# A transformer layer with routed experts on one core: gate and up in three passes of split numbers, small VectorE work moved to ScalarE and GpSimd

## The chip, the cores and the metric

One NeuronCore of a Trainium2 chip runs the whole layer as one program. Its engines run side by side and meet at semaphores: TensorE (PE) multiplies, VectorE (DVE) and ScalarE (ACT) work on SBUF and PSUM, GpSimd (POOL) on SBUF, SyncE (SP) issues most DMAs. The metric is device time in microseconds, lower is better. Three runs of the kernel before took 2507.96, 2511.35 and 2512.93 us, median 2511.35.

## The reference

The input x has shape 8 x 1024 x 256, float32. The layer is attention with a residual and a layer norm, then a routed feed-forward with a residual and a layer norm.

```python
q = einsum('bld,dhk->blhk', x, Wq)            # 16 heads of 64
latent = einsum('bld,dc->blc', x, Wkv_down)   # 64 wide
k, v = latent @ Wk_up, latent @ Wv_up         # per head
attn = softmax(where(causal, q @ k.T / 8, min))
x = layernorm(x + (attn @ v) @ Wout)
# routed feed-forward: T = 8192 tokens, E = 32 experts, C = 320 slots each
probs = softmax(xt @ w_router); top1 = argmax(probs); gate = probs[top1]
pos = cumsum(onehot(top1))[top1] - 1          # rank among the expert's tokens
buf[top1 * C + pos] = xt                      # dropped where pos >= C
g, u = buf @ w_gate, buf @ w_up               # 256 x 256 per expert
y = (silu(g) * u) @ w_down
x = layernorm(xt + where(pos < C, y[slot] * gate, 0))
```

## The kernel before

**Attention.** The loop runs over 64 pairs of heads (gp, eight per batch b, p = gp % 8) and in each over 12 slots t, a slot being 128 keys against a block of 512 queries. In a slot TensorE makes scores by keys (`turned_scores`, L699 and L702), scores by rows for the row maxima of the next pair (`row_scores`, L674), and every second slot probabilities times values (`values`, L722). VectorE takes the row maxima (`row_max`, L1117 and L1121), ScalarE the exponentials (L964), GpSimd masks the diagonal (L479) and adds up the probabilities (L494 to L504). Every engine's program is written out in one order by hand. What belongs to the batch before is put between the slots of the next batch's first pairs: output projection in p = 0 and 1, layer norm in p = 1 and 2, transposed rows and router logits in p = 2, ranks in p = 3, sending rows to the experts' slots in DRAM in p = 4 and 5. The layer norm's steps are `variance` (VectorE, L1191 and L1194), `roots` (GpSimd, L517 to L529) and `normalise` (VectorE, L1199: x1 minus mean, times rstd, four tiles of 128 x 256 at slots (1, 10) and (2, 4)). `count_tiles` (L1240 to L1244) and `destinations` (L1249 to L1257) are VectorE's work in p = 3, slots 9 and 11; `send` (L536) is GpSimd's indirect DMA.

TensorE's float32 products come as two instructions in the trace. Products in F32R come as one; where float32 accuracy is wanted with them, an operand is split into a high part (a cast to F32R) and a low part (the rest), and three passes are added: high by high, low by high, high by low. Queries and latents are made in that way (L621).

**Experts.** When all rows are in DRAM, the loop runs over 32 experts, two to a pair g. TensorE transposes an expert's 320 rows (`transpose_rows`, L879), VectorE copies them to SBUF (`copy_rows`, L1332 and L1333), TensorE makes gate and up in float32 (`gate_and_up`, L891), ScalarE applies silu (`activate`, L1038), VectorE multiplies (`hidden`, L1338), TensorE projects down in five blocks of 128 rows per pair (`down`, L910 and L915), VectorE adds them to the rows and takes their statistics (`add_to_rows`, L1350 to L1364), GpSimd takes the root (`root`, L572 and L575), ScalarE scales (`normalise_out`, L1044), and GpSimd sends the rows to the output (`send_back`, L581). TensorE's order is gate and up of e, transposes of e+2, and after the second expert of a pair the down projection. ScalarE's is the activations of e and, after those of a pair's first expert, `normalise_out` of the pair before.

Weights have eight buffers (`ex_w`, AHEAD = 8), `ex_y` two. SP loads the weights of five experts during the last pair of heads, the other three between the first rows, and then for e = 8 and on:

```python
for e in range(AHEAD, E):
    g = (e - AHEAD) // 2
    sp.wait_ge(ex_sent[g % 2], 16 * NY * (g // 2 + 1))   # output of pair g has landed
    load_rows(e)
    load_weights(e)                                      # gate, up, down: three DMAs
```

Of the kernel before, what the change touches and what calls it, by code (L numbers as in the profile page):

```python
# [16 lines left out]
P = 128  # L17
# [6 lines left out]
def build_layer(nc, x, Wq, Wkv, Wk_up, Wv_up, Wout, w_router, w_gate, w_up, w_down, out):  # L24
# [48 lines left out]

    NADD = 11
# [7 lines left out]
    with ExitStack() as ctx:  # L82
# [23 lines left out]
        fold_lo = sb("fold_lo", [P, KD, NPAIR * P], F32R, attn)  # L106
        future = sb("future", [P, BANK], F32, attn)
# [6 lines left out]
        lat_hi = [sb(f"lat_hi{i}", [P, L], F32R, attn) for i in range(2)]  # L114
        lat_lo = [sb(f"lat_lo{i}", [LD + 1, L], F32R, attn) for i in range(2)]
        lat_keys = [sb(f"lat_keys{i}", [P, NT, LD], F32, attn) for i in range(2)]
        fold_v = sb("fold_v", [P, NPAIR, D], F32, attn)
        q_hl = [sb(f"q_hl{i}", [P, 2, L], F32R, attn) for i in range(2)]
# [52 lines left out]
        EARLY_W = 5  # L171
# [6 lines left out]
        ex_xT = sb("ex_xT", [P, 2, KD, 2 * C], F32, tail)  # L178
# [40 lines left out]
        rstd_ready = sem("rstd_ready")  # L219
        x1_ready = sem("x1_ready")  # L220
# [10 lines left out]
        ex_loaded = [sem(f"ex_loaded{i}") for i in range(AHEAD)]  # L231
        ex_t_full = sem("ex_t_full")
# [34 lines left out]
        for gp in range(PAIRS):  # L267
# [16 lines left out]
            if b and p == 2:  # L284
                for use, t in zip([(hf, kd) for hf in range(2) for kd in range(KD)], (3, 5, 7, 10)):
                    late[t].append(("x1T", b - 1, *use))
                late[11].append(("logits", b - 1))
# [71 lines left out]
        def _(sp):  # L359
# [42 lines left out]
            def load_weights(e):  # L402
                k = e % AHEAD
                for m, w in enumerate((w_gate, w_up, w_down)):
                    sp.dma_start(ex_w[k][:, m], w[e].rearrange("(k p) f -> p k f", p=P)).then_inc(ex_loaded[k], 16)
# [37 lines left out]
        def _(pool):  # L443
# [69 lines left out]
            def roots(b, hf):  # L513

                tiles = slice(hf * HPB, (hf + 1) * HPB)
                pool.wait_ge(var_ready, b * 2 + hf + 1)
                nc.gpsimd.tensor_tensor(rstd[:, tiles], var_eps[:, tiles], minus_half[:, tiles], ALU.pow  # L517
                                        ).then_inc(rstd_ready, 1)
                pool.wait_ge(rstd_ready, b * 2 + hf + 1)
                nc.gpsimd.tensor_tensor(alone[:, 0, tiles], rstd[:, tiles], rstd[:, tiles], ALU.mult  # L520
# [9 lines left out]
                                        ).then_inc(alone_scale, 1)  # L530

# [8 lines left out]
            for gp in range(PAIRS):  # L540
                b, p = divmod(gp, NPAIR)
                for t in range(NSLOT):
# [10 lines left out]
                    if b and (p, t) in ((1, 8), (2, 2)):  # L553
# [6 lines left out]
            for hf in range(2):  # L560
                roots(LAST, hf)
            for i in range(NT):
                send(LAST, i)
# [4 lines left out]
            def root(g):  # L568

                part = slice(g % 2 * NY, (g % 2 + 1) * NY)  # L570
                pool.wait_ge(var_ready, 2 * B + g + 1)
                nc.gpsimd.tensor_tensor(rstd[:, part], var_eps[:, part], minus_half[:, part], ALU.pow  # L572
# [13 lines left out]

            for g in range(E // 2):
                root(g)
                send_back(g)

        @block.tensor
        def _(pe):
# [181 lines left out]
            def count(b):  # L774
                use = ("pos", b)
                bank = take(use)
                pe.wait_ge(onehot_ready, b + 1)
                nc.tensor.matmul(bank[:, 0:NT * E], before_bf[:, :], onehot[:, :, :].rearrange("p t e -> p (t e)"),
# [89 lines left out]
            def transpose_rows(e):  # L868
# [3 lines left out]
                if u == 0:  # L872
                    for k in (e % AHEAD, e % AHEAD + 1):
                        pe.wait_ge(ex_loaded[k], (e // AHEAD + 1) * (16 * (3 + NB)))
# [8 lines left out]
            def gate_and_up(e):  # L883
                g, u = divmod(e, 2)
                pe.wait_ge(ex_t_ready, e + 1)
                for f in range(KF):
                    if e:
                        pe.wait_ge(ex_h_ready[f], e)
                    for m in range(2):
                        for kd in range(KD):  # L890
                            mm = nc.tensor.matmul(turned_ps[f][:, m, 0:C], ex_w[e % AHEAD][:, m, kd, f * P:(f + 1) * P],  # L891
                                                  ex_xT[:, g % 2, kd, u * C:(u + 1) * C],
                                                  start=(kd == 0), stop=(kd == KD - 1))
# [36 lines left out]
        def _(act):  # L930
# [42 lines left out]

            def pass_alone(b, i):
# [36 lines left out]

            for gp in range(PAIRS):
                b, p = divmod(gp, NPAIR)
                for t in range(NSLOT):
# [5 lines left out]
                    for use in EARLY.get((gp, t), []) + LATE[gp, t]:  # L1020
                        if use[0] in STAGES:
                            STAGES[use[0]](*use[1:])
                    if b and p == 3 and t < NT:
                        pass_alone(b - 1, t)
                    if b and (p, t) == (3, 4):
                        gate_exponentials(b - 1)
            copy_heads(PAIRS - 1, 1)
# [11 lines left out]

            def normalise_out(g):  # L1040
# [6 lines left out]

            for e in range(0, E, 2):
                for u in range(2):
                    activate(e + u)  # L1050
                    if e and u == 0:
                        normalise_out(e // 2 - 1)
            normalise_out(E // 2 - 1)

        @block.vector
        def _(dve):
# [130 lines left out]
            def variance(b, hf):  # L1187
                tiles = slice(hf * HPB, (hf + 1) * HPB)
# [3 lines left out]
                step(last)  # L1192
                settle()
                nc.vector.tensor_scalar(var_eps[:, tiles], mean_var[:, tiles, 1], EPS, None, ALU.add).then_inc(var_ready, 1)  # L1194

            def normalise(b, hf):
                dve.wait_ge(rstd_ready, b * 2 + hf + 1)
                for i in range(hf * HPB, (hf + 1) * HPB):
                    last = nc.vector.tensor_scalar(x1[:, i, 0:D], x1[:, i, 0:D], mean_var[:, i, 0:1], rstd[:, i:i + 1],  # L1199
                                                   ALU.subtract, ALU.mult)  # L1200
                last.then_inc(x1_ready, 1)
# [36 lines left out]
            def count_tiles(b):  # L1238
# [3 lines left out]
                step(nc.vector.tensor_tensor(earlier[:, :, :], earlier[:, :, :],  # L1242
                                             in_tiles[:, :].unsqueeze(1).to_broadcast([P, NT, E]), ALU.add))
                step(nc.vector.reciprocal(rt[:, 2, :], rt[:, 1, :]))  # L1244

            def destinations(b):

                settle()
                step(nc.vector.scalar_tensor_tensor(rt[:, 5, :], rt[:, 3, :], float(C), rt[:, 4, :], ALU.mult, ALU.add))  # L1249
                step(nc.vector.tensor_scalar(rt[:, 7, :], rt[:, 4, :], float(C), FAR, ALU.is_ge, ALU.mult))  # L1250
                settle()
                step(nc.vector.scalar_tensor_tensor(rt[:, 8, :], rt[:, 5, :], float(SLOTS), rt[:, 7, :], ALU.add, ALU.add))
                nc.vector.tensor_scalar(x1[:, :, GATE], rt[:, 2, :], 0.5, None, ALU.mult)
                step(nc.vector.tensor_copy(x1[:, :, TOKEN].bitcast(I32), token_f[:, :]))
                settle()
                nc.vector.tensor_scalar(token_f[:, :], token_f[:, :], float(L), None, ALU.add).then_inc(routed, 1)
                nc.vector.tensor_copy(send_idx[:, :], rt[:, 8, :]).then_inc(send_ready, 1)  # L1257
# [28 lines left out]
            for gp in range(PAIRS):  # L1286
                b, p = divmod(gp, NPAIR)
                for t in range(NSLOT):
# [15 lines left out]
                    if b and (p, t) == (3, 11):  # L1304
                        destinations(b - 1)
                    if b and (p, t) in ((1, 5), (2, 0)):
                        variance(b - 1, p - 1)
                    if b and (p, t) in ((1, 10), (2, 4)):
                        normalise(b - 1, p - 1)
            for use in ENDING:  # L1310
# [5 lines left out]
                if use[0] == "pos":  # L1316
                    count_tiles(LAST)
                    destinations(LAST)
                if use[0] == "rest" and use[2] == HPB - 1:
                    variance(LAST, 0)  # L1320
                if use[0] == "rest" and use[2] == NT - 1:
                    normalise(LAST, 0)
                    variance(LAST, 1)
                    normalise(LAST, 1)

            def copy_rows(e):
# [5 lines left out]
                nc.vector.tensor_copy(ex_xT[:, g % 2, 0, cols], ex_ring[0][:, 0:width])  # L1332
                nc.vector.tensor_copy(ex_xT[:, g % 2, 1, cols], ex_ring[1][:, 0:width]).then_inc(ex_t_ready, 1)  # L1333
# [62 lines left out]
```

## Time and profile before

| | us |
|---|---|
| median of three runs | 2511.35 |
| profiled execution, its own time | 2510.11 |
| span of the profiled execution | 2508.0 |
| busy: PE, DVE, ACT, POOL | 2345.6, 1602.7, 1015.1, 1678.9 |
| attention, up to the last batch's router | to about 2210 |
| first transposes of experts' rows | 2248.4 |

The span runs from the program's first to its last instruction; the time of a run has a little around it. Busy time alone says little, since the engines overlap: the chain that ended last tells which of them set the end, the idle time in front of an instruction tells what it waited for, and a timeline of one round shows the order.

### The profile page before, as it was taken

How to read it: one execution, taken by the hardware profiler on the slowest of the kernel's cores; microseconds unless marked ns; L12 is line 12 of the kernel's file. 1: busy time of each engine (PE TensorE's matmuls, PEld its weight loads, DVE VectorE, ACT ScalarE, POOL GpSimd, SP SyncE). 2: the span in 40 equal slices, each digit the busy share in tenths (PEclk: the TensorE clock that was granted, in tenths of full speed). 3: DMA queues.
4: the chain of work that ended last, by engine and by line, in shares of the span. 5: the costliest groups of instructions: out<-in, count | busy, mean ns of one | idle time of the engine just before them, and what ended most of it. 6: DMA issues, size and time to landing. Idle time of an engine off the chain costs nothing.

```text
span 2508.0 us, 36804 instructions
## 1 busy us (share of the span) xinstructions
PE 2345.6 (94%) x11528; PEld 1517.6 (61%) x11528; DVE 1602.7 (64%) x4618; ACT 1015.1 (40%) x1992; POOL 1678.9 (67%) x1623
## 2 busy tenths in 40 slices
PE   6999999999999999999999999999999999949996
PEld 4555575556655665566555665566556655537774
DVE  4677657765676667765776567666776577335553
ACT  3445424443444334542444334433444344212222
POOL 1688756975787757875797568766787579623444
PEclk8999999999999999999999999999999999969998
DMA  3222100200011001100020001100110001224652
GB/s 87 60 64 81 39 14 14 73 18 14 18 49 37 18 10 39 47 18 13 18 69 18 14 18 51 35 18 9 43 43 18 18 14 55 68 79 155 193 180 68
DMA packets 96818, 118.96 MB, mean 47 GB/s; under 512 B 12289, under 2 KB 75783, under 8 KB 96625
## 3 DMA queue, kind: packets, MB, share of 16 engines
q1 hardware_dynamic: 89712, 99.98, 14.5%
q0 software_dynamic: 6912, 16.64, 1.9%
q8 instruction: 93, 1.52, 0.2%
q14 instruction: 101, 0.82, 0.1%
HBM read 46.91 MB, written 37.90 MB: 34 GB/s over the span
## 4 chain that ended last, share of the span: by engine, by line
PE 76%; DVE 13%; issue 6%; POOL 1%; ACT 1%; DMA 0%; DVEq 0%; SPq 0%; POOLq 0%; ACTq 0%
PE value_ps L722 18%; PE misc_ps L744 9%; PE turned_ps L699 9%; PE turned_ps L702 8%; PE misc_ps L621 8%; PE turned_ps L891 6%; PE row_ps L674 6%; PE turned_ps L674 3%; PE misc_ps L734 3%; DVE masked_row L1117 2%; DVE q_hl L1098 2%; DVE q_hl L1097 2%; DVE rinv L1151 1%; PE misc_ps L770 1%; DVE x L1199 1%
## 5 line engine op out<-in xcount | busy, mean ns | idle before, releaser
L964 ACT ACTIVATE probs<-turned_ps 128x512 f32<-128x512 f32 (+2 forms) x1280 | 652.1, 554 | 815.2 <-PE turned_ps L702 801.2
L504 POOL TENSOR_TENSOR half_sums<-half_sums,probs 128x1024 f32<-128x1024 f32 (+3 forms) x512 | 832.4, 1626 | 33.2 <-ACT probs L964 15.9
L722 PE MATMUL value_ps<-probs,lat_keys 128*64 128x512 f32 (+3 forms) x3072 | 597.7, 511 | 0.0
L699 PE MATMUL turned_ps<-q_hl,lat_hi 128*128 128x512 f32 (+2 forms) x1280 | 529.7, 414 | 1.5 <-ACT fold_v L1009 1.5
L702 PE MATMUL turned_ps<-q_max,lat_lo 65*128 65x512 f32 (+2 forms) x1280 | 483.7, 378 | 2.5 <-DMA q_max<-both_rows 2.5
L479 POOL TENSOR_SCALAR_AFFINE_SELECT probs<-probs 128x256 f32<-128x256 f32 x512 | 210.3, 411 | 405.0 <-ACT probs L964 404.1
L1117 DVE CUSTOM_DVE_ANT_0 masked_row<-row_ps,future 128x512 bf16<-128x512 f32 (+4 forms) x707 | 347.3, 511 | 189.6 <-PE row_ps L674 184.2
L499 POOL TENSOR_TENSOR half_sums<-probs 128x768 f32<-128x768 f32 (+1 forms) x128 | 269.4, 2105 | 140.8 <-ACT probs L964 118.2
L674 PE MATMUL row_ps<-lat_hi,q_hl 128*128 128x512 f32 (+4 forms) x1026 | 324.3, 356 | 33.0 <-DVE neg_max L1117 18.5
L722 PEld LDWEIGHTS value_ps<-probs,lat_keys 128*64 128x64 f32 x3072 | 190.5, 139 | 265.3 <-issue 199.8
L699 PEld LDWEIGHTS turned_ps<-q_hl,lat_hi 128*128 128x128 f32 x1280 | 244.6, 191 | 137.3 <-issue 107.9
L702 PEld LDWEIGHTS turned_ps<-q_max,lat_lo 65*128 65x128 f32 x1280 | 246.3, 192 | 31.8 <-DMA q_max<-both_rows 3.0
L674 PEld LDWEIGHTS row_ps<-lat_hi,q_hl 128*128 128x128 f32 x1026 | 193.5, 194 | 86.5 <-DVE neg_max L1117 29.9
L744 PE MATMUL misc_ps<-fold_v,headsT 128*128 128x256 f32 x1008 | 232.4, 383 | 8.8 <-DVE q_hl L1098 4.7
L1121 DVE TENSOR_REDUCE unit_max<-row_ps 128x1 f32<-128x512 f32 (+1 forms) x319 | 200.0, 643 | 37.1 <-PE row_ps L674 36.8
L744 PEld LDWEIGHTS misc_ps<-fold_v,headsT 128*128 128x128 f32 x1008 | 187.3, 190 | 53.8 <-issue 13.2
L674 PE MATMUL turned_ps<-lat_hi,q_hl 128*128 128x320 f32 x510 | 177.6, 348 | 17.6 <-DVE unit_max L1121 13.4
L511 POOL TENSOR_TENSOR headsT<-headsT,rinv_rows 128x512 f32<-128x512 f32 x128 | 164.3, 1284 | 37.6 <-DVE rinv_rows L1155 37.4
L1117 DVE CUSTOM_DVE_ANT_0 masked_row<-turned_ps,future 128x256 bf16<-128x256 f32 (+1 forms) x317 | 160.7, 507 | 23.5 <-PE turned_ps L674 23.1
L944 ACT CAST q_hl<-misc_ps 64x512 fp32r<-64x512 f32 x125 | 72.6, 581 | 242.5 <-PE misc_ps L621 242.5
L891 PE MATMUL turned_ps<-ex_xT,ex_w 128*128 128x320 f32 x512 | 146.6, 440 | 0.0
L1121 DVE TENSOR_REDUCE unit_max<-turned_ps 128x1 f32<-128x512 f32 (+1 forms) x193 | 119.5, 619 | 22.8 <-PE turned_ps L674 13.8
(191 smaller groups left out, 2652.3 us busy)
## 6 DMA issues: line engine op xcount, KB each, us to landing
q_max<-q_hl SPq DMA_DIRECT2D x256, 128.0 KB
slots_x<-router SPq DMA_DIRECT2D x8, 1290.0 KB, 6.0
ex_x<-slots_x SPq DMA_DIRECT2D x64, 129.0 KB, 2.4
x_in<-in_L_attn_x_bld SPq DMA_DIRECT2D x8, 1024.0 KB, 5.5
layer_out<-x_in SPq DMA_DIRECT2D x8, 1024.0 KB, 4.5
ex_w<-in_L_ffn_w_gate SPq DMA_DIRECT2D x32, 256.0 KB, 3.7
ex_w<-in_L_ffn_w_up SPq DMA_DIRECT2D x32, 256.0 KB, 3.8
ex_w<-in_L_ffn_w_down SPq DMA_DIRECT2D x32, 256.0 KB, 4.3
```

The lines of the kernel that those rows point to most:

```text
L479: nc.gpsimd.affine_select(out=block, in_=block, pattern=[[0, 2], [1, P]], compare_op=ALU.is_ge, fill=0.0, base=0, channel_multiplier=-1).t ...
L499: nc.gpsimd.tensor_tensor(sums_of(gp, c)[:, :, q0:BANK], before[:, :, q0:BANK], now[:, :, q0:BANK], ALU.add).then_inc(added, 1)
L504: nc.gpsimd.tensor_tensor(total, total, now[:, :, q0:BANK], ALU.add).then_inc(added, 1)
L674: nc.tensor.matmul(dst[:, 0:k1 - k0], q_hl[gp % 2][:, h, i * P:(i + 1) * P], lat_hi[b % 2][:, k0:k1], start=True, stop=True).then_inc(rows ...
L699: nc.tensor.matmul(scores_of(n, h), lat_hi[b % 2][:, keys], q_hl[gp % 2][:, heads, cols], start=True, stop=False)
L702: nc.tensor.matmul(scores_of(n, h), lat_lo[b % 2][:, keys], q_max[:, c, heads, q0:BANK], start=False, stop=True).then_inc(turned_full, 1)
L722: mm = nc.tensor.matmul(value_ps[h * LD:(h + 1) * LD, q0:BANK], lat_keys[b % 2][:, j, :], probs[:, n % NPROBS, h, q0:BANK], start=(j == 0) ...
L744: mm = nc.tensor.matmul(bank[:, 0:D], headsT[:, (NPAIR * b + j) % NHEADS, i * P:(i + 1) * P], fold_v[:, j, :], start=(j == 0), stop=(j == ...
L891: mm = nc.tensor.matmul(turned_ps[f][:, m, 0:C], ex_w[e % AHEAD][:, m, kd, f * P:(f + 1) * P], ex_xT[:, g % 2, kd, u * C:(u + 1) * C], sta ...
L964: nc.scalar.activation(probs[:, n % NPROBS, heads, q0:BANK], scores_of(n, h), ACT.Exp).then_inc(exp_done, 1)
L1117: nc.vector.tensor_tensor_reduce(masked_row[n % 2][:, 0:width], row[:, 0:width], future[:, BANK - width:], scale=-1.0, scalar=-MASKED, op0 ...
L1121: nc.vector.tensor_reduce(dst, row[:, 0:width], AX.X, ALU.max, negate=True).then_inc(max_done, 1)
```

## The change

1. Gate and up of an expert become three passes in F32R: high weights by high rows, low by high, high by low. ScalarE casts the weights (`high_weights`) and the transposed rows (`high_rows`); GpSimd subtracts for the low weights (`low_weights`), VectorE for the low rows (`copy_rows`). There are four buffers of split weights. Three experts' weights are loaded and split during the last pair of heads instead of five loaded.
2. In the experts' loop, statistics come after the next pair's first hidden product (`row_statistics`), `normalise_out` after the second activation instead of the first, and eps and the negated mean move from VectorE to GpSimd.
3. In attention, `normalise` moves to ScalarE, tile by tile (`normalise_tile`), except in the last batch; eps and shift move to GpSimd (`roots`), one slot earlier; `destinations` and the running count (`earlier`) move to GpSimd, at slot (4, 3); the sends move to p = 5 and 6. Buffers of the attention stage are allocated in another order, so that the new ones lie on dead ones.

```diff
+    NORMALISE_AT = [(1, 9), (1, 10), (1, 11), (2, 0), (2, 4), (2, 5), (2, 6), (2, 6)]
-        EARLY_W = 5
+        NWH = 4
+        EARLY_W = 3
+        EARLY_SPLIT = (7, 9, 11)
 # GpSimd
+                nc.gpsimd.tensor_scalar(var_eps[:, tiles], mean_var[:, tiles, 1], EPS, None, ALU.add).then_inc(eps_added, 1)
+                nc.gpsimd.tensor_scalar(rt[:, 9, tiles], mean_var[:, tiles, 0], -1.0, None, ALU.mult).then_inc(eps_added, 1)
...
+            def destinations(b):
+                pool.wait_ge(counted, b + 1)
...
+                if b < LAST:
+                    nc.gpsimd.tensor_tensor(earlier[:, :, :], earlier[:, :, :],
+                                            in_tiles[:, :].unsqueeze(1).to_broadcast([P, NT, E]), ALU.add
+                                            ).then_inc(earlier_ready, 1)
...
-                    if b and p in (4, 5) and t < HPB:
-                        send(b - 1, (p - 4) * HPB + t)
+                    if b and (p, t) == (4, 3):
+                        destinations(b - 1)
+                    if b and p in (5, 6) and t < HPB:
+                        send(b - 1, (p - 5) * HPB + t)
...
+            def low_weights(e):
+                pool.wait_ge(ex_wh_done, e + 1)
+                nc.gpsimd.tensor_tensor(ex_wl[e % NWH][:, :, :, :], ex_w[e % AHEAD][:, 0:2],
+                                        ex_wh[e % NWH][:, :, :, :].bitcast(F32), ALU.subtract).then_inc(ex_wl_done, 1)
...
+            low_weights(EARLY_W)
             for g in range(E // 2):
+                for e in (2 * g + NWH, 2 * g + NWH + 1):
+                    if e < E:
+                        low_weights(e)
                 root(g)
                 send_back(g)
 # TensorE, gate_and_up
+                pe.wait_ge(ex_wl_done, e + 1)
+                wh, wl = ex_wh[e % NWH], ex_wl[e % NWH]
+                passes = [(w, x, kd) for w, x in ((wh, ex_xh), (wl, ex_xh), (wh, ex_xl)) for kd in range(KD)]
 # ScalarE
+            def normalise_tile(b, i):
+                act.wait_ge(x1_shift_ready, b * 2 + i // HPB + 1)
+                ins = nc.scalar.activation(x1[:, i, 0:D], x1[:, i, 0:D], ACT.Identity,
+                                           bias=rt[:, 6, i:i + 1], scale=rstd[:, i:i + 1])
...
+            def high_weights(e):
+                k = e % AHEAD
+                act.wait_ge(ex_w_loaded[k], 48 * (e // AHEAD + 1))
+                nc.scalar.copy(ex_wh[e % NWH][:, :, :, :], ex_w[k][:, 0:2]).then_inc(ex_wh_done, 1)
...
+            def high_rows(e):
+                act.wait_ge(ex_t_full, e + 1)
...
+                for kd in range(KD):
+                    nc.scalar.copy(ex_xh[:, g % 2, kd, cols], ex_ring[kd][:, 0:width]).then_inc(ex_xh_done, 1)
...
+            for u in range(2):
+                high_rows(u)
+            for e in range(EARLY_W, NWH):
+                high_weights(e)
             for e in range(0, E, 2):
                 for u in range(2):
                     activate(e + u)
-                    if e and u == 0:
+                    if e + u + 2 < E:
+                        high_rows(e + u + 2)
+                    if e and u == 1:
                         normalise_out(e // 2 - 1)
+                    if e + u + NWH < E:
+                        high_weights(e + u + NWH)
 # VectorE
-                step(nc.vector.tensor_tensor(earlier[:, :, :], earlier[:, :, :],
-                                             in_tiles[:, :].unsqueeze(1).to_broadcast([P, NT, E]), ALU.add))
...
-                    if b and (p, t) in ((1, 10), (2, 4)):
-                        normalise(b - 1, p - 1)
...
                 for u in range(2):
                     hidden(e + u)
+                    if e and u == 0:
+                        row_statistics(e // 2 - 1)
                     if e + u + 2 < E:
                         copy_rows(e + u + 2)
                 add_to_rows(e // 2)
```

## Rows read from the trace of the kernel before

**Rows 1.** The page: busy time of the engines; the chain that ended last, by engine.
```profile
PE 2345.6 (94%) x11528; PEld 1517.6 (61%) x11528; DVE 1602.7 (64%) x4618; ACT 1015.1 (40%) x1992; POOL 1678.9 (67%) x1623
...
PE 76%; DVE 13%; issue 6%; POOL 1%; ACT 1%; DMA 0%; DVEq 0%; SPq 0%; POOLq 0%; ACTq 0%
```
**Rows 2.** Timelines of VectorE and TensorE (start, length, instruction [idle before it <- releaser]), fifth batch.
```profile
1196.54 3.86 DVE L1199 TENSOR_SCALAR x<-x,mean_var,rstd 128x256 f32<-128x256 f32 x4
...
1200.85 0.50 PE L674 MATMUL row_ps<-lat_hi,q_hl 128*128 128x512 f32 x1 [1.97 <-DVE unit_max L1117]
...
1249.39 1.16 DVE L1242 TENSOR_TENSOR earlier<-earlier,in_tiles 128x256 bf16<-128x256 bf16 x1
...
1251.44 0.50 PE L674 MATMUL turned_ps<-lat_hi,q_hl 128*128 128x512 f32 x1 [1.52 <-DVE unit_max L1121]
```
**Rows 3.** Windows: length; busy PE, PEld, DVE, ACT, POOL; granted clock, DMA share, GB/s.
```profile
2300.00:2400.00 100.00, 99.77 (x454) 71.49 (x454) 54.96 (x170) 28.87 (x63) 43.99 (x49) 1.00 0.61 193
```
**Rows 4.** Timeline of all engines over one pair of experts.
```profile
2282.16 0.97 POOL L581 DMA_INDIRECT layer_out<-ex_y,ex_x  x1 [0.30 <-issue]
...
2284.41 0.81 SPq L412 DMA_DIRECT2D ex_x<-slots_x  x2
...
2286.38 1.20 POOL L572 TENSOR_TENSOR rstd<-var_eps,minus_half 128x5 f32<-128x5 f32 x1 [3.24 <-DVE var_eps L1364]
...
2286.91 0.47 SPq L405 DMA_DIRECT2D ex_w<-in_L_ffn_w_down  x1
...
2287.90 0.44 ACT L1038 ACTIVATE ex_s<-turned_ps 128x320 f32<-128x320 f32 x1 [1.72 <-PE turned_ps L891]
2288.24 2.55 ACT L1044 ACTIVATE ex_y<-ex_y,shift,rstd 128x256 f32<-128x256 f32 x5
...
2288.36 4.47 PE L891 MATMUL turned_ps<-ex_xT,ex_w 128*128 128x320 f32 x16
...
2291.60 1.04 POOL L581 DMA_INDIRECT layer_out<-ex_y,ex_x  x1 [3.75 <-ACT ex_y L1044]
...
2292.67 0.60 PE L879 MATMUL row_ps<-ident,ex_x 128*128 128x128 f32 x4
...
2296.78 0.97 POOL L581 DMA_INDIRECT layer_out<-ex_y,ex_x  x1 [0.31 <-issue]
```
**Rows 5.** Transfers: the down matrices, median us to landing; all loads of weights (L405).
```profile
ex_w<-in_L_ffn_w_down SPq DMA_DIRECT2D x32, 256.0 KB, 4.3
...
DMA to landing us min/median/max: 2.8/3.9/7.3
```
**Rows 6.** Timeline of ScalarE: the first and the last of 16 scalings of output blocks.
```profile
2273.59 0.59 ACT L1044 ACTIVATE ex_y<-ex_y,shift,rstd 128x256 f32<-128x256 f32 x1
...
2491.68 2.56 ACT L1044 ACTIVATE ex_y<-ex_y,shift,rstd 128x256 f32<-128x256 f32 x5 [8.63 <-POOL shift L575]
```
**Rows 7.** Timeline of TensorE: two F32R products of 320 columns in a row.
```profile
1196.81 0.31 PE L674 MATMUL row_ps<-lat_hi,q_hl 128*128 128x320 f32 x1
1196.96 0.31 PE L674 MATMUL turned_ps<-lat_hi,q_hl 128*128 128x320 f32 x1
```
**Rows 8.** Groups by line and shape: count, busy us, mean ns, idle before and its releasers.
```profile
L504 POOL TENSOR_TENSOR half_sums<-half_sums,probs 128x1024 f32<-128x1024 f32 x192 | 456.8, 2379 | 24.1 <-ACT probs L964 15.9
...
L964 ACT ACTIVATE probs<-turned_ps 128x384 f32<-128x384 f32 x256 | 111.8, 489 | 153.7 <-PE turned_ps L702 152.7
...
L933 ACT CAST xT_hi<-misc_ps 128x512 fp32r<-128x512 f32 x28 | 16.4, 587 | 24.9 <-PE misc_ps L631 24.7
```
**Rows 9.** Timeline of GpSimd and VectorE: small instructions in the last batch.
```profile
2208.32 0.24 POOL L526 TENSOR_SCALAR alone<-alone 128x4 f32<-128x4 f32 x1
...
2230.11 0.17 DVE L1249 SCALAR_TENSOR_TENSOR rt<-rt 128x8 f32<-128x8 f32 x1
...
2230.84 0.16 DVE L1257 CAST send_idx<-rt 128x8 int32<-128x8 f32 x1
```
**Rows 10.** Windows, columns as in rows 3: TensorE's clock behind the idle of 1.97 us.
```profile
1201.60:1205.00 3.40, 3.40 (x16) 2.50 (x13) 2.67 (x9) 1.53 (x3) 1.14 (x1) 0.50 0.01 1
```

More of the change, by code:

```diff
@@ L219, in build_layer @@
         rstd_ready = sem("rstd_ready")
+        eps_added = sem("eps_added")
+        x1_shift_ready = sem("x1_shift_ready")
+        counted = sem("counted")
+        earlier_ready = sem("earlier_ready")
+        route_step = sem("route_step")
         x1_ready = sem("x1_ready")
@@ L889, in gate_and_up @@
                     for m in range(2):
[L890 to L893, printed above, removed]
+                        for n, (w, x, kd) in enumerate(passes):
+                            mm = nc.tensor.matmul(turned_ps[f][:, m, 0:C], w[:, m, kd, f * P:(f + 1) * P],
+                                                  x[:, g % 2, kd, u * C:(u + 1) * C],
+                                                  start=(n == 0), stop=(n == len(passes) - 1))
                     mm.then_inc(ex_g_full, 1)
@@ L1022, in _ @@
                             STAGES[use[0]](*use[1:])
+                    for i, at in enumerate(NORMALISE_AT):
+                        if b and (p, t) == at:
+                            normalise_tile(b - 1, i)
                     if b and p == 3 and t < NT:
@@ L1026, in _ @@
                         gate_exponentials(b - 1)
+                    if gp == PAIRS - 1 and t in EARLY_SPLIT:
+                        high_weights(EARLY_SPLIT.index(t))
             copy_heads(PAIRS - 1, 1)
@@ L1191, in variance, with normalise @@
                     last = nc.vector.bn_aggr(mean_var[:, i, :], stat6[:, i, :])
[L1192 to L1198, printed above, removed]
+                last.then_inc(var_ready, 1)
+            def normalise(b, tiles):
+                for i in tiles:
+                    dve.wait_ge(rstd_ready, b * 2 + i // HPB + 1)
                     last = nc.vector.tensor_scalar(x1[:, i, 0:D], x1[:, i, 0:D], mean_var[:, i, 0:1], rstd[:, i:i + 1],
                                                    ALU.subtract, ALU.mult)
-                last.then_inc(x1_ready, 1)
+                    if i % HPB == HPB - 1:
+                        last.then_inc(x1_ready, 1)
             over = lambda k: rt[:, k, :].unsqueeze(2).to_broadcast([P, NT, E])
@@ L1360, in add_to_rows @@
                     last = nc.vector.bn_aggr(mean_var[:, g % 2 * NY + n, :], stat6[:, g % 2 * NY + n, :])
[L1361 to L1365 removed]
+                last.then_inc(var_ready, 1)
             for u in range(2):
```

93 lines of the change are left out of this document (59 added, 34 removed).

## Prediction

> **What bounds the kernel now.** I read the page first: the busy line, then the chain that ended last [rows 1]. TensorE is busy for 94% of the span and holds 76% of the chain; VectorE holds 13%, GpSimd 1%. So a moved instruction is worth something only where TensorE waits for VectorE. The change touches two stages, and I read each from its own rows. In attention the timeline shows two places per batch where TensorE stands still for VectorE: 1.97 us behind the four normalising instructions of L1199, which take 3.86 us, and 1.52 us behind the counting (L1240 to L1244), of which L1242 alone takes 1.16 us [rows 2]. In the experts' stage a stretch of 100 us has TensorE busy for 99.8 us at full clock, with DMA at 0.61 [rows 3]. The timeline of one pair of experts [rows 4] shows who else is in the round: ScalarE scales the five output blocks, GpSimd sends them, and their landing lets SP load the next rows and weights into the same buffers. That ring has slack: SP starts on expert 8 at 2284.41, its weights are there by 2291.2 [rows 4, 5], and TensorE wants them in pair 4, near 2310. One round takes (2491.68 - 2273.59) / 15 = 14.54 us [rows 6]. The question is whether the slack outlives the change.
>
> **Gate and up, on TensorE.** Before: 16 records in 2292.67 - 2288.36 = 4.31 us per expert [rows 4]. After: 24 matmuls of 320 columns with F32R operands. L674 issues just such ones 0.15 us apart [rows 7]: 24 x 0.15 = 3.6 us. That removes 0.7 us per expert, 22.7 us over 32, if TensorE goes on setting the pace (if the weight loads don't hide, nothing). A pair would then last 14.54 - 1.4 = 13.1 us.
>
> **The splitting, on the other engines.** Per pair ScalarE gets two copies of 1024 columns (high_weights) and four of 384 or 256 (high_rows). A copy of 512 takes 0.587 us, an exponential of 384 0.489 [rows 8]; their slope gives 0.98 us for 1024 and 0.39 for 256, plain doubling 1.17 for 1024. I take 1.0, since the two rows show a fixed part. GpSimd gets two subtractions of 1024 columns at 2.38 us [rows 8] and two small instructions of 0.24 [rows 9] in the root. By busy time both fit into 13.1 us: ScalarE 4 x 0.44 + 2.55 + 2 x 1.0 + 1.8 = 8.1, GpSimd 6.15 + 2 x 2.38 + 2.0 = 12.9. They don't fit by order.
>
> **The wait that appears.** high_weights(e) stands in ScalarE's queue right behind the activations of expert e-4 and the rows of e-2, and waits until the weights of e have landed. These are loaded when the output of pair (e-8)/2 has landed, because e and e-8 share a buffer; SP's loop is unchanged. So the weights are wanted two pairs earlier than before, while normalise_out moves one activation later. For pair g the ring, from the start of normalise_out(g), by [rows 4]: five scalings 2.55; from their end at 2290.79 to the first send at 2291.60, 0.81; to the start of the fifth at 2296.78, 5.18; landing and SP's wake 2284.41 - 2282.16 = 2.25; SP's issues up to the down matrix 2286.91 - 2284.41 = 2.50; its landing 4.3 [rows 5] (all three matrices must be there). Together 17.6 us. Then high_weights 1.0, the two activations queued behind it 2 x 0.44, high_rows 2 x 0.39, and only then normalise_out(g+1) in the same queue: 2.8 us with the semaphores. The ring is 20.4 us, against 13.1 for TensorE. ScalarE stands for some 8 us in every round; behind it wait the activation, the hidden product, the down projection and the next gate and up, so TensorE stands too. It recurs for the weights of experts 8, 10, ... 30: 12 rounds from normalise_out(0) to normalise_out(12), 245 us. The last three have no weights to wait for, and GpSimd sets them: 2.55 + 0.81 + 5.18 + 0.97 for scaling and sends, 2 x 2.38 for the last subtractions, 2.0 for the root (1.20 of it the power [rows 4]): 16.3, then twice 11.6. Sum 284.5 us against 218.1 before [rows 6]: **+66 us**. Landings range from 2.8 to 7.3 us [rows 5], which makes the ring 18.9 to 23.4 and the sum +48 to +102; the mean of many rounds lies near the median.
>
> **The start of that stage.** normalise_out(0) waits for two more gate-and-ups and their high rows (9.2 us) where it waited for statistics and root (4.2); the shorter products give 1.4 back, the two-step split of the first rows costs 0.6: +4 us. destinations on GpSimd is on the path in the last batch only. VectorE's run goes from 2230.11 to 2231.00 [rows 9]; eight GpSimd instructions at 0.24 with their waits are 2.3. With earlier gone from VectorE, and eps on GpSimd twice: +1.5 us (0.5 to 3). The three early low_weights run on GpSimd under the router's logits, 7.2 us in a longer idle: nothing. Weights 3 and 4 now load behind rows; rows 0 to 3 keep their place in SP's queue: nothing.
>
> **Attention.** Per batch the 1.97 us go, because normalising is on ScalarE, eight instructions of 0.5 us over eight slots. Behind such an idle TensorE is granted half its clock, 1.2 GHz, for a stretch [rows 10]: 3.4 us at 0.50 lose up to 1.7. Of the 1.52 us, 1.16 go with L1242, and up to 1.7 of clock again. At most 6.5 us per batch, 46 us over 7 batches; at least zero, if something else is late at once. Late next is ScalarE: its new pieces stand ahead of exponentials whose banks TensorE wants back, perhaps 0.5 us per batch. Some of what is lost at half clock is time that TensorE would lose to other waits anyway. I take two thirds, 4.3 per batch: **-30 us**. The GpSimd additions (roots 0.75 us twice, destinations 3 us) fit into its idle time, a third of the span [rows 1]. The sends move from pairs 4 and 5 to 5 and 6 at the same load per slot. The waits earlier_ready on TensorE and x1_shift_ready on ScalarE are met many slots before: nothing.
>
> **Sum.** 66 + 4 + 1.5 - 30 = +42 us on the profiled execution's 2510.11 us (span 2508.0), which is 1.2 below the median of 2511.35. **2552 us.**
>
> **Rivals.** (a) Faster: the weights land before ScalarE asks. TensorE stays the pace: -22.7 + 5.5 - 30 gives 2463. It decides in the ring: from normalise_out to landed weights would have to fit into 13.1 - 2.8 = 10.3 us, and the rows add to 17.6, the five sends alone being half of 10.3. For it speaks TensorE's 99.8% [rows 3]. 6%.
> (b) GpSimd is the pace: scaling, sends, two subtractions and root in one queue, 16.3 us. That needs the landing to be hidden but not the queue. 13 rounds of 16.3 and two of 11.6 are 235 against 218: +17, with + 5.5 - 30 that is 2503. 6%.
> (c) TensorE at half clock: 5 to 7 us of new idle in each round, where 1.97 sufficed for a stretch at 0.50 [rows 2, 10]. Between a late hidden product and the next asked weights it has three down blocks (2.7), two gate-and-ups (7.2) and two transposes (1.1) to do, 11 us in about 18. Wholly at 1.2 GHz they are 22, and the ring becomes 1.4 + 22 + 1.2 = 24.6: 12 x 4.2 more, 2602. Against it: the stage's dense work runs at full clock [rows 3], and one idle brought one stretch, not a lasting state. 9%. The Trainium skill, "TensorE: Matmul & The Clock Gate", section "HAM oscillation — how this bites in real kernels", warns of just this: a loop that waits for a transfer in each round has its array throttled again in each. Rows 10 agree for a single idle; no row here shows a loop of them.
> (d) Attention gives nothing back, its waits being filled at once: 2582, the forecast's upper edge.
>
> **How the numbers follow.** The forecast, with (d) as its edge, has 79% and 2528 to 2583 as its own range (landings +-0.7 us over 12 rounds are +-8; attention -12 to -44; the start 3 to 8). Outside 2520 to 2590 lie (a), (b), half of (c) and a little of the forecast: about 19%. What can be told from no change is 0.2%, 5 us. Faster: (a), (b) and an attention gain near its bound with a short ring, 13%. Same: 4%. Slower: 83%.
>
> **What would show it.** Right, if the profile after has: gate and up as 24 records in about 3.6 us; ScalarE idle before high_weights with a load of ex_w as releaser, some 8 us in each of twelve rounds; 20.4 us between starts of normalise_out; the idle of 1.97 us and its half clock gone from the second and third pair of a batch. Wrong, if rounds are near 13 (a), near 16.3 with GpSimd busy throughout (b), or if the granted clock in the experts' stage is near 0.5 and TensorE without idle (c). The attention term is wrong if the time up to the last batch's router shrinks by less than 12 us or more than 44.

## The result, and the profile after

The changed kernel takes 2533.77 us (median of 4 runs, 2532.23 to 2534.49); the kernel before, timed beside it on the same chip, 2509.65 (2506.58 to 2512.93). The ratio is 1.0095, interval 1.0078 to 1.0113: slower by 24 us, where 41 were forecast. The profiled execution took 2533.69 us, its span is 2531.9.

The two spans, 2508.04 and 2531.92, differ by 23.9 us. Cut at four events that both traces have, they give the whole account:

| stretch | forecast | measured |
|---|---|---|
| start to the first head copy of the last pair, ScalarE's copy of finished values (2156.11, after 2115.57) | -30 | -40.5 |
| last pair, router, sends, to the first transposes of experts' rows (2248.41, after 2210.07) | +1.5 | +2.2 |
| to the start of normalise_out(0) (25.18 long, after 28.46) | +4 | +3.3 |
| normalise_out(0) to normalise_out(15) (218.1 long, after 276.9) | +66 | +58.8 |
| to the end of the span (16.36, after 16.47) | 0 | +0.1 |
| sum | +41.5 | +23.9 |

The page of after, busy time and the chain that ended last (answers to [rows 1]):

```profile
PE 2325.6 (92%) x11784; PEld 1538.1 (61%) x11784; DVE 1520.1 (60%) x4450; ACT 1092.4 (43%) x2144; POOL 1790.9 (71%) x1806
...
PE 67%; DVE 10%; issue 7%; POOL 4%; ACT 4%; DMA 3%; SPq 1%; POOLq 0%; DVEq 0%; ACTq 0%
```

VectorE's share of the chain went from 13% to 10%: in attention it holds 69 us less. DMA, ScalarE and GpSimd, 2% together before, hold 11%, most of it in the experts' stage, where TensorE holds 17 of 322 us of the chain; before it held 237 of 260. Which DMA it is, the longest pieces of the chain tell (start, length, what):

```profile
2212.51 4.44 DMA ex_w<-in_L_ffn_w_down
...
2251.95 4.08 DMA ex_w<-in_L_ffn_w_down
...
2468.82 4.18 DMA ex_w<-in_L_ffn_w_down
```

There are twelve of them from 2251.95 to 2468.82, one per round: the landing of the down matrix is on the path in each, as the forecast's ring has it. From the first scaling on, the chain does not pass through TensorE at all. The window in mid-stage (columns as in [rows 3]) has TensorE busy for 78 us of 100 where it had been 99.8, at a granted clock of 0.86:

```profile
2300.00:2400.00 100.00, 78.24 (x417) 64.82 (x415) 39.27 (x116) 37.85 (x77) 59.68 (x57) 0.86 0.45 138
```

ScalarE's timeline, with the first scaling, the sixth after it and the last (answers to [rows 6]):

```profile
2238.53 2.57 ACT L1141 ACTIVATE ex_y<-ex_y,shift,rstd 128x256 f32<-128x256 f32 x5
...
2356.03 2.09 ACT L1141 ACTIVATE ex_y<-ex_y,shift,rstd 128x256 f32<-128x256 f32 x4
...
2515.45 2.57 ACT L1141 ACTIVATE ex_y<-ex_y,shift,rstd 128x256 f32<-128x256 f32 x5 [9.27 <-POOL shift L636]
```

The round that begins at 2356.03, all engines (answers to [rows 4]):

```profile
2359.41 1.11 POOL L642 DMA_INDIRECT layer_out<-ex_y,ex_x  x1 [5.95 <-ACT ex_y L1141]
...
2363.01 0.71 PE L961 MATMUL turned_ps<-ex_xh,ex_wh 128*128 128x320 f32 x2
...
2364.66 0.98 POOL L642 DMA_INDIRECT layer_out<-ex_y,ex_x  x1 [0.30 <-issue]
...
2366.79 0.82 PE L946 MATMUL row_ps<-ident,ex_x 128*128 128x128 f32 x6
2366.95 0.81 SPq L434 DMA_DIRECT2D ex_x<-slots_x  x2
...
2369.45 0.48 SPq L426 DMA_DIRECT2D ex_w<-in_L_ffn_w_down  x1
...
2371.53 1.03 PE L980 MATMUL value_ps<-ex_w,ex_h 128*128 128x256 f32 x4
...
2373.51 1.04 ACT L1093 CAST ex_wh<-ex_w 128x1024 fp32r<-128x1024 f32 x1 [5.00 <-DMA ex_w<-in_L_ffn_w_down]
2374.46 0.76 ACT L1126 ACTIVATE ex_s<-turned_ps 128x320 f32<-128x320 f32 x2
...
2375.11 0.65 ACT L1135 CAST ex_xh<-row_ps 128x256 fp32r<-128x256 f32 x2
2375.62 2.57 ACT L1141 ACTIVATE ex_y<-ex_y,shift,rstd 128x256 f32<-128x256 f32 x5
...
2377.01 2.05 PE L980 MATMUL value_ps<-ex_w,ex_h 128*128 128x256 f32 x4 [3.59 <-DVE ex_y L1437]
```

Read it as a circle: scaling at 2356.03, first send 2359.41, fifth 2364.66, SP wakes at 2366.95 and issues the down matrix at 2369.45, it lands, high_weights runs at 2373.51, and behind it in the same queue two activations, two high rows and the next scaling at 2375.62. That is 3.38 + 5.25 + 2.29 + 2.50 + 4.06 + 2.11 = 19.59 us, the distance between the scalings.

### The profile page after: what moved, and what is told of

Same layout as the page of the kernel before. It is cut to its first block, busy times and chain, and to the rows that moved or that the text cites. A ratio compares the mean times of both kernels' runs of the same rounds, so it can differ in the third digit from the quotient of the medians.

```text
span 2531.9 us, 37516 instructions
## 1 busy us (share of the span) xinstructions
PE 2325.6 (92%) x11784; PEld 1538.1 (61%) x11784; DVE 1520.1 (60%) x4450; ACT 1092.4 (43%) x2144; POOL 1790.9 (71%) x1806
## 3 DMA queue, kind: packets, MB, share of 16 engines
q0 software_dynamic: 6912, 16.64, 1.9%
## 4 chain that ended last, share of the span: by engine, by line
PE 67%; DVE 10%; issue 7%; POOL 4%; ACT 4%; DMA 3%; SPq 1%; POOLq 0%; DVEq 0%; ACTq 0%
PE value_ps L787 18%; PE misc_ps L809 9%; PE turned_ps L764 9%; PE turned_ps L767 8%; PE misc_ps L686 8%; PE row_ps L739 5%; PE turned_ps L739 3%; PE misc_ps L799 2%; POOL layer_out L642 2%; DVE q_hl L1203 2%; DMA ex_w<-in_L_ffn_w_down 2%; DVE masked_row L1222 2%; DVE q_hl L1202 2%; ACT ex_y L1141 2%; DVE rinv L1256 1%
## 5 line engine op out<-in xcount | busy, mean ns | idle before, releaser
L787 PE MATMUL value_ps<-probs,lat_keys 128*64 128x512 f32 (+3 forms) x3072 | 589.9, 505 | 1.3 <-POOL probs L501 1.3
L1014 ACT CAST q_hl<-misc_ps 64x512 fp32r<-64x512 f32 x125 | 72.6, 580 | 234.8 <-PE misc_ps L686 234.8
L642 POOL DMA_INDIRECT layer_out<-ex_y,ex_x x80 | 80.2, 1002 | 110.9 <-ACT ex_y L1141 91.4
L1284 DVE TENSOR_TENSOR x<-misc_ps,x_in 128x256 f32<-128x256 f32 x64 | 27.2, 425 | 182.2 <-PE misc_ps L809 182.2
```

The costliest lines, as they stand in the source:

```text
L787: mm = nc.tensor.matmul(value_ps[h * LD:(h + 1) * LD, q0:BANK], lat_keys[b % 2][:, j, :], probs[:, n % NPROBS, h, q0:BANK], start=(j == 0) ...
```

## The experiments

**Each part alone.** The attention part on the kernel before, experts untouched (NORMALISE_AT, eps and shift on GpSimd, destinations and earlier on GpSimd, sends one pair later):

> The kernel before with the attention and routing part of the change alone; experts as before. If the gain of attention and the loss of the experts' stage add up: the time up to the experts' first transposes falls by 38 us as it does in the kernel after (2248.4 to 2210.1), rounds stay 14.65, so about 2509.7 - 38 = 2472 us. Rival: the attention gain comes from somewhere the experts' part of the change touches (the buffers' order, fewer early loads): then less than 30 us of gain, over 2480.

Measured: 2471.64 us (2470.97 to 2472.74), ratio 0.9858 (0.9841 to 0.9874). Its rounds are 14.65 us as before (the mean of 14.54 that the prediction took has a shorter last round in it). So the attention part is worth -36 us, and the experts' part takes 62 in the full change.

Half of the attention part: only normalising moves.

```diff
+ NORMALISE_AT = [(1, 9), (1, 10), ...]     # normalise_tile on ScalarE, eps and shift on GpSimd
  # count_tiles, destinations and sends as in the kernel before
```

> The kernel before with only this edit: normalise on ScalarE in single tiles, eps and shift on GpSimd one slot earlier; counting, destinations and sends stay as before, and so do the experts. Theory (the gain in attention is two separate waits of TensorE on VectorE): the second pair of a batch falls from 40.8 to 38.5 us and the third by about 1, the fourth stays at 31.4: 7 x 3.3 = 23 us less at most, 16 at least, 2484 to 2492. The counting part then holds the rest of the 36 us of the whole attention edit. Rival (the two hang together, the later wait being left over from the earlier one): most of the 36 us go already here, 2475 or less.

Measured: 2492.13 us (2487.02 to 2492.96), ratio 0.9923 (0.9905 to 0.9941), against 2509.79 of the kernel before on that chip: -18, at the upper end of the expected times. Of the -36 that leaves about -18 for the counting, by difference; the counting alone was not run. TensorE's waits in the fifth batch of this run (timeline; idle and releaser in brackets) show the first nearly gone and the other in place, so the two gains are separate:

```profile
1196.25 0.63 PE L774 MATMUL misc_ps<-ident,x 128*128 128x128 f32 x4 [0.40 <-ACT x L989]
...
1241.23 0.50 PE L686 MATMUL turned_ps<-lat_hi,q_hl 128*128 128x512 f32 x1 [1.52 <-DVE unit_max L1144]
```

**Is it the ring?** Three edits of the changed kernel, each at another place of the circle. First, GpSimd takes the root ahead of the two subtractions:

```diff
 for g in range(E // 2):
+    root(g)
     for e in (2 * g + NWH, 2 * g + NWH + 1):
         if e < E: low_weights(e)
-    root(g)
     send_back(g)
```

> The kernel after, with GpSimd's root ahead of the two low_weights of each round instead of behind them. Ring of the weights (scaling, sends, landing, loads, split on ScalarE): the root is no part of it, so rounds stay at 19.5 us and the total within 5 us of 2533.8; only the rounds without loads at the end get up to 3 us shorter. GpSimd's queue as the bound: the two subtractions (4.8 us) move under ScalarE's scaling and rounds shrink by some 3 us, to 16.5: about 2495.

Measured: 2535.23 us (2532.87 to 2538.70), ratio 1.0109 (1.0092 to 1.0126), no change. The order of subtractions and root on GpSimd is not on the ring. The waits of this run (us in total, times, longest):

```profile
ACT ex_wh L1093 <- DMA ex_w<-in_L_ffn_w_down: 74.9, 12, 11.2
POOL neg_mean L630 <- DVE mean_var L1451: 61.9, 13, 15.8
```

ScalarE still waits for weights in twelve rounds; GpSimd now waits earlier, for VectorE's statistics.

Second, SP issues weights ahead of rows:

```diff
-                load_rows(e)
                 load_weights(e)
+                load_rows(e)
```

> The kernel after, with SP issuing an expert's weights ahead of its rows. Ring of the weights: the three issues of the rows (1.35 us) leave it in each of 12 rounds, 19.5 becomes about 18.2, total down by 16 us to about 2518. GpSimd's queue or TensorE at half clock as the bound: no change, 2533.8, or a little slower, since rows come later.

Measured: 2516.28 us (2515.08 to 2519.01), ratio 1.0035 (1.0021 to 1.0050). The twelve rounds average 18.1 us (19.7 in the changed kernel), 1.6 us less. SP's issues of the rows, which left the circle, take 1.35 of that in the changed kernel (from 2366.95 to the first issue of weights at 2368.30). Third, the scaling goes back to the pair's first activation, ahead of the wait, and the statistics right behind add_to_rows:

```diff
                 add_to_rows(e // 2)
+                row_statistics(e // 2)
...
                     activate(e + u)
+                    if e and u == 0:
+                        normalise_out(e // 2 - 1)
                     if e + u + 2 < E:
                         high_rows(e + u + 2)
-                    if e and u == 1:
-                        normalise_out(e // 2 - 1)
```

> The kernel after, with statistics and scaling back where they were before (statistics right behind add_to_rows, scaling behind the activations of a pair's first expert). Ring of the weights: scaling then stands ahead of the blocked high_weights in ScalarE's queue instead of behind it, the ring spans two rounds (about 27.5 us for two) and no longer decides; GpSimd's queue does, at about 16.3 us per round: 13 x 16.3 + 23 against 277 us, total near 2494. If the place of the scaling does not matter (the loads are late by themselves): rounds stay at 19 to 20, total within 8 us of 2533.8. TensorE at half clock: no change.

Measured: 2497.59 us (2494.84 to 2499.44), ratio 0.9960 (0.9947 to 0.9972). Most rounds are 16.64 us, and ScalarE's wait for weights is no longer among its long ones. In their place:

```profile
POOL layer_out L642 <- ACT ex_y L1141: 54.6, 16, 3.5
ACT ex_y L1141 <- POOL shift L636: 35.4, 16, 9.0
```

Scaling and GpSimd wait for each other: that is rival (b)'s bound.

**Without the ring.** Gate and up get their own loads, four experts earlier, as soon as the split that read the buffer is done; rows and the down matrix stay behind the landed output. Gate and up of experts 8 to 11 are loaded ahead of this loop.

```diff
             for e in range(AHEAD, E):
                 ...
                 load_rows(e)
-                load_weights(e)
+                load_down(e)
+                if e + 4 < E:
+                    sp.wait_ge(ex_wl_done, e + 4 - AHEAD + 1)
+                    load_gate_up(e + 4)
```

> The gate and up matrices of an expert get their own loads, issued four experts earlier, as soon as the split of the expert that held the buffer is done; only rows and the down matrix still wait for the landed output. Theory (the ring through the weights sets the round): ScalarE's wait for loads of ex_w goes, and what is left is GpSimd's queue (scaling, five sends, two subtractions, root), 16.6 us per round as in the run that scaled early: 13 rounds of 16.6 and two of 11.8 against 12 of 19.6 give about 36 us less, 2497 (2490 to 2506). Rival (the stage's pace is the bound by other things, such as TensorE at half clock or the rows' own loads): rounds stay near 19.5 and the time near 2534.

Measured: 2495.61 us (2494.27 to 2498.61), ratio 0.9944 (0.9927 to 0.9962). Thirteen rounds between 16.55 and 16.67 us, then 11.84 and 11.81. GpSimd's timeline has one round in it:

```profile
2342.11 1.11 POOL L654 DMA_INDIRECT layer_out<-ex_y,ex_x  x1 [3.41 <-ACT ex_y L1153]
...
2348.35 4.66 POOL L626 TENSOR_TENSOR ex_wl<-ex_w,ex_wh 128x1024 fp32r<-128x1024 f32 x2
...
2355.05 0.20 POOL L648 TENSOR_TENSOR shift<-neg_mean,rstd 128x5 f32<-128x5 f32 x1
2358.65 1.12 POOL L654 DMA_INDIRECT layer_out<-ex_y,ex_x  x1 [3.41 <-ACT ex_y L1153]
```

Sends, subtractions, root, and then 3.41 us in which ScalarE scales and GpSimd stands: 16.54 us. The root's place in the queue, worth nothing while the ring was there, should now count:

> As the run with early loads of gate and up, and GpSimd takes the root of a pair before the two subtractions, so that scaling no longer waits for them. Theory (GpSimd's queue by its order is the next bound, not its work): its busy time is 12.9 us per round and TensorE's 13.1, rounds of 13.1 to 13.9 where TensorE sets the pace: NO(0) to NO(15) about 205 us against 276.9, 2455 to 2468. Rival 1 (GpSimd's work itself is the bound, with VectorE's statistics ahead of the root): 15 to 16.6 per round, 2480 to 2497. Rival 2 (order of GpSimd does nothing, as when the ring was in place): 2497.

Measured: 2459.21 us (2457.93 to 2460.46), ratio 0.9797 (0.9779 to 0.9814). Rounds average 13.4 us (13.25 to 14.91, the last 11.83). GpSimd's timeline and the window in mid-stage:

```profile
2362.64 0.20 POOL L648 TENSOR_TENSOR shift<-neg_mean,rstd 128x5 f32<-128x5 f32 x1
2362.80 4.69 POOL L626 TENSOR_TENSOR ex_wl<-ex_w,ex_wh 128x1024 fp32r<-128x1024 f32 x2
2367.65 1.12 POOL L654 DMA_INDIRECT layer_out<-ex_y,ex_x  x1 [0.16 <-issue]
```
```profile
2300.00:2400.00 100.00, 96.41 (x604) 84.12 (x603) 57.23 (x166) 54.94 (x110) 84.39 (x82) 1.00 0.63 197
```

The scaling now runs under the subtractions, GpSimd's idle of 3.41 us ahead of the sends is 0.16, and TensorE is back at 96 us of 100 and full clock. This version beats both kernels. Against the run with the attention part alone it is 12 us faster: its rounds take 16.8 us less in sum, its start 3.2 more. That is what the three passes are worth here once the two circles are cut; most of the rest is attention's.

**Is the later scaling then needed?** The same with statistics and scaling early, as in the third edit above:

> Early loads, root first, and statistics and scaling where the kernel before has them (right behind the down projection; scaling behind the pair's first activation). Theory (the later scaling is only worth something where TensorE would wait for VectorE's statistics): with scaling one activation earlier each chain is shorter, rounds of 13.1 to 13.9, 2452 to 2468, within 8 us of the run with root first alone. Rival (statistics ahead of the low rows delay gate and up on TensorE, and ScalarE waits for the root): rounds of 14.5 or more, 2475 or above.

Measured: 2471.68 us (2471.26 to 2471.91), ratio 0.9848 (0.9830 to 0.9866), rounds of 14.6: a miss. The rounds are the rival's, the time lies between the two. The timeline shows why:

```profile
2353.55 2.57 ACT L1153 ACTIVATE ex_y<-ex_y,shift,rstd 128x256 f32<-128x256 f32 x5 [0.73 <-POOL shift L648]
...
2356.02 0.83 ACT L1147 CAST ex_xh<-row_ps 128x384 fp32r<-128x384 f32 x2
...
2356.58 1.02 DVE L1430 TENSOR_TENSOR ex_xl<-row_ps,ex_xh 128x384 fp32r<-128x384 f32 x2 [3.24 <-ACT ex_xh L1147]
...
2357.66 0.66 PE L958 MATMUL row_ps<-ident,ex_x 128*128 128x128 f32 x4 [1.14 <-DVE ex_xl L1430]
```

The high rows stand behind five scalings, so VectorE's low rows and TensorE's transposes wait. One more run put only these two the other way round:

```diff
                     activate(e + u)
-                    if e and u == 0:
-                        normalise_out(e // 2 - 1)
                     if e + u + 2 < E:
                         high_rows(e + u + 2)
+                    if e and u == 0:
+                        normalise_out(e // 2 - 1)
```

> As the run with early loads, root first and early scaling (rounds of 14.6), but ScalarE makes the high rows of e+2 ahead of the five scalings. Theory (that run's rounds came from the low rows of VectorE, which waited 3.3 us in each round for high rows standing behind the scalings): the wait of 1.14 us of TensorE's transposes goes, and that of the activation behind; rounds of 13.3 to 13.8 and 2456 to 2464, equal within 5 us to early loads with root first alone. Rival (statistics right behind the down projection, ahead of the hidden product on VectorE, cost the round): rounds stay at 14.6, 2472.

Measured: 2461.95 us (2459.79 to 2462.52), ratio 0.9811 (0.9795 to 0.9827). The time is in the expected range, the rounds are not: 14.1 us, where 13.3 to 13.8 were expected. The wait of the transposes is gone, but TensorE now waits elsewhere:

```profile
2361.55 1.02 DVE L1430 TENSOR_TENSOR ex_xl<-row_ps,ex_xh 128x384 fp32r<-128x384 f32 x2 [0.28 <-ACT ex_xh L1147]
...
2365.59 0.88 DVE L1437 TENSOR_TENSOR ex_h<-ex_s,turned_ps 128x320 f32<-128x320 f32 x2 [3.02 <-ACT ex_s L1138]
...
2367.68 0.67 PE L992 MATMUL value_ps<-ex_w,ex_h 128*128 128x256 f32 x2 [1.06 <-DVE ex_y L1449]
```

The second activation stands behind the scalings and a split of weights, and the hidden product and the down projection behind it. Of the 7.3 us that the longer rounds cost, 4.7 are won back at the start, where the first scaling comes 23.3 us after the first transposes and not 28.0 as in the run with early loads and root first. The two intervals overlap, so the two versions can't be told apart. What counted was that the scalings don't stand ahead of the high rows (9 to 10 us, 8 of them in the rounds); whether they come one activation later is worth no time that was measured here, once the ring is gone.

## Why the prediction was right, and where its sizes were off

**The sign and the mechanism were right.** The step that decided was "They don't fit by order": the weights wanted two pairs earlier, the scaling behind the wait for them in ScalarE's queue, the reload behind the scaling's output. The runs cut this ring at two separate places, the loads and the scaling's place in the queue (with the statistics), and either cut brought back some 36 to 38 us; shortening it by SP's issues alone brought 1.6 us per round; and the edit off the ring brought nothing. It recurred in twelve rounds, and the last two rounds were 11.86 and 11.83 us against 11.6. Two rivals named the next bounds at nearly their size: GpSimd's queue (16.3 forecast, 16.55 measured; 2503 forecast, 2495.6 measured) and TensorE as the pace (2463 forecast, 2459.2 measured), once their conditions were made. That their totals came so near has luck in it: ahead of the experts' stage these runs won 7 to 8 us more than the two sums held, and their rounds cost 4 to 6 us more.

**Gate and up.** Forecast 24 records in 3.6 us. In the round shown, from 2363.01 to the transposes at 2366.79, 3.78. The splits cost what was taken (groups by line: min, median, max in ns):

```profile
L1093 ACT CAST ex_wh<-ex_w x32: 1029/1044/1083, 2117.3 to 2477.6; 128x1024 fp32r<-128x1024 f32 x32
...
L614 POOL TENSOR_TENSOR ex_wl<-ex_w,ex_wh x32: 2342/2406/2427, 2175.1 to 2487.1; 128x1024 fp32r<-128x1024 f32 x32
```

**The ring's size.** Forecast 20.4 us, measured 19.5 as the mean of the first eleven. The twelfth was 21.7, since its output took 4.24 us to land, where the chain has 2.05 to 2.31 in the others:

```profile
2462.06 4.24 DMA layer_out<-ex_y,ex_x
```

Two terms were too large: the down matrix landed in 4.06 and not 4.3, and the piece behind it took 2.11 and not 2.8. There I had added up durations (1.0, 2 x 0.44, 2 x 0.39); in the timeline each instruction of ScalarE starts before the one ahead has ended in the trace (2373.51, 2374.46, 2375.11, 2375.62). Starts, not durations, are to be added within a queue. ScalarE's wait was 72.6 us in twelve, 6.0 each and not some 8:

```profile
ACT ex_wh L1093 <- DMA ex_w<-in_L_ffn_w_down: 72.6, 12, 8.1
```

**Attention was the mis-sized term: -30 forecast, -40.5 measured.** The step that failed was "I take two thirds" of "at most 6.5 us per batch". From the first head copy of the second batch to that of the last pair, which takes in the seven batches that follow the first, the gain is 41.5 us, 5.9 per batch, so the bound held in sum and the cut was wrong (0.9 us more pass ahead of the first batch's copies). The fifth batch, which the prediction read, gains most. Its second, third and fourth pair, from first head copy to first head copy, before and after (columns as in [rows 3]):

```profile
1161.43:1202.64 41.21, 38.58 (x192) 26.10 (x191) 28.86 (x79) 14.62 (x28) 30.16 (x32) 0.99 0.06 14
1202.64:1238.53 35.89, 35.58 (x176) 23.09 (x176) 22.45 (x65) 17.23 (x35) 20.02 (x21) 0.87 0.07 16
1238.53:1269.97 31.44, 29.46 (x145) 17.21 (x145) 25.70 (x72) 14.10 (x28) 27.16 (x26) 0.95 0.13 35
```
```profile
1144.05:1182.64 38.59, 37.91 (x192) 25.95 (x192) 22.48 (x70) 17.47 (x34) 28.65 (x37) 1.00 0.07 15
1182.64:1216.46 33.82, 33.11 (x176) 21.06 (x176) 22.85 (x66) 17.82 (x37) 22.73 (x22) 0.95 0.07 17
1216.46:1244.77 28.31, 27.55 (x145) 16.78 (x145) 21.43 (x64) 14.11 (x29) 24.84 (x31) 1.00 0.09 20
```

The three pairs lose 7.8 us. TensorE's idle time (length less busy) falls from 4.92 to 2.15, which is 2.8; the other 5.0 are busy time, with the same 192, 176 and 145 records. That is the clock: the share missing from full speed times the length is 6.6 us before (0.01 x 41.21 + 0.13 x 35.89 + 0.05 x 31.44) and 1.7 after. Over all seven batches TensorE's idle time falls by 20.3 us and what the clock loses by 20.5; the bound had 21.9 and 23.8. So both sizes were near. Rows 10 were not typical, though: the idle of 1.97 us stands in all seven batches, and a stretch at half clock goes with it in two of them alone, the fourth and the fifth. The waits behind the counting are followed by one in all seven. The reason for the cut, that other waits would take the time, did not hold: the rests of the two idles of [rows 2] are small.

```profile
1184.36 0.63 PE L827 MATMUL misc_ps<-ident,x 128*128 128x128 f32 x4 [0.39 <-ACT x L1047]
...
1228.32 0.50 PE L739 MATMUL turned_ps<-lat_hi,q_hl 128*128 128x512 f32 x1 [0.44 <-DVE unit_max L1226]
```

The forecast had put a late ScalarE at 0.5 us per batch, by way of the exponentials. The first line has TensorE wait 0.39 us for ScalarE, but for the normalised rows themselves. The granted clock in that pair, 0.95, is still not full, so the last sign that the forecast named is met in part; the reason is another one (last section).

**Half clock (rival c) came, and cost nothing.** The four matmuls of a down block took 2.05 us behind the idle of 3.59 (2377.01) and 1.03 in the dense stretch (2371.53), and the stage's clock was 0.86. But the ring ran through ScalarE, GpSimd, SyncE and DMA, the chain that ended last has no piece of TensorE in any of these rounds, and TensorE's slower products fitted into its wait: the round was 19.6 us, not 24.6. The Trainium skill, "TensorE: Matmul & The Clock Gate", section "HAM oscillation — how this bites in real kernels", says that a loop which waits for a transfer in each round has its array throttled again in each; the rows agree. That the rule bears on the time only if TensorE is in the ring, the rows add.

**The start of the stage** was +3.3 for +4, and the router's part with the last pair +2.2 for +1.5. One edit of the start that was costed at nothing is on the chain, though: the landing at 2212.51 is that of expert 3's weights, which load behind rows now. ScalarE stood 1.89 us for them ahead of its first activation, and a table load of 1.28 us (ACT_TABLE_LOAD) that lay in ScalarE's idle time before follows it on the chain. TensorE stood 0.82 us behind that.

## What to carry to other kernels

When work is moved ahead of a wait, or a wait ahead of work, in one engine's queue, draw the circle: who refills the buffer that is waited for, what releases the refill, and whether that release now stands behind the wait. Add the circle up from start to start and hold it against the busiest engine; busy times alone said that this change fits. And cure the longest circle first: the same edit of GpSimd's order was worth nothing with the ring in place and 36 us without it.

## What was not expected of the hardware

- The clock fell where TensorE did not stand, too. In the third pair of the fifth batch 0.13 of the clock were missing over 35.89 us. Most of it is a stretch at 0.50 that begins at 1218.6, while TensorE works off the router's logits, more than 17 us behind its last idle of over 0.1 us. After the change each of the seven batches has one such stretch, during or right behind the logits, and up to the last pair no other; in the fifth batch it makes the 0.95. That the logits cause it was not tested. Logits (timeline of TensorE) and stretch (columns as in [rows 3]), before and after:

```profile
1215.53 4.24 PE L770 MATMUL misc_ps<-wr,x1T 128*128 128x32 f32 x32
1218.60:1225.40 6.80, 6.80 (x23) 3.88 (x23) 3.47 (x11) 1.59 (x3) 2.89 (x4) 0.50 0.01 2
```
```profile
1195.01 3.76 PE L835 MATMUL misc_ps<-wr,x1T 128*128 128x32 f32 x32
1199.40:1202.80 3.40, 3.40 (x12) 1.40 (x10) 3.06 (x10) 1.59 (x3) 2.10 (x3) 0.50 0.02 5
```

- VectorE's four normalising instructions took 3.86 us in the fifth batch [rows 2], while GpSimd ran additions of up to 1024 columns, and 1.36 us in the last batch, where GpSimd had only small ones. ScalarE's took 0.60 each. Of all 64 such instructions 28 took over 0.45 us, up to 2.46, and each of the 28 overlaps an addition of 256 columns or more on GpSimd; the longest of the fifth batch ran from 1197.95 to 1200.39, GpSimd's addition of 1024 columns beside it from 1197.84 to 1200.24. That GpSimd's work was the cause was not tested by a run. The Trainium skill, "GPSIMD Engine Reference", section "8. Key points", says that GpSimd shares its SBUF interfaces with VectorE, and that VectorE instructions with two SBUF inputs or in a two-port mode contend with it; the overlaps fit that, but no row shows whether these instructions were of that kind, and no run here isolates it. The kernel before, the last batch in VectorE's timeline and all instructions of the line (min, median, max in ns):

```profile
2209.10 1.36 DVE L1199 TENSOR_SCALAR x<-x,mean_var,rstd 128x256 f32<-128x256 f32 x4
...
L1199 DVE TENSOR_SCALAR x<-x,mean_var,rstd x64: 395/424/2455, 368.9 to 2213.0; 128x256 f32<-128x256 f32 x64
```
